# Scores of the 129-key row block in 64x128 tiles, and an earlier wait for the scores made ahead

## What is computed

```python
xn = layernorm(x, g_in)
q = (xn @ Wq).reshape(b, n, H, DH).transpose(0, 2, 1, 3) * scale
k, v = split(xn @ Wkv)
k = concatenate([nk, k]); v = concatenate([nv, v])      # 129 keys
sim = einsum('bhid,bjd->bhij', q, k) + bias             # the scores
sim = where(causal_mask, neg, sim)
attn = softmax(sim)
out = einsum('bhij,bjd->bhid', attn, v).reshape(b, n, INNER) @ Wo
return layernorm(out, g_out)
```

## Time and profile before

| | us |
|---|---|
| median of 3 runs | 2392.63 |
| lowest and highest run | 2391.18, 2395.41 |
| the profiled execution's own time | 2398.92 |
| span of its trace, first to last instruction | 2397.1 |
| PE busy | 2148.4 (90%) |
| PEld busy | 1914.7 (80%) |
| DVE busy | 1624.3 (68%) |
| ACT busy | 1557.8 (65%) |
| POOL busy | 1030.0 (43%) |
| mean granted clock of PE | 0.957 |

### The profile page before, as it was taken

One profiled execution on the slowest core, in us unless ns is written; L12 is line 12 of the kernel. 1 busy time (PEld: TensorE's weight loads), 2 busy tenths in 40 slices (PEclk: granted clock), 3 DMA queues, 4 the chain that ended last, 5 costly groups with the idle time before them and its releaser, 6 DMA issues.

```text
span 2397.1 us, 72132 instructions
## 1 busy us (share of the span) xinstructions
PE 2148.4 (90%) x26395; PEld 1914.7 (80%) x26395; DVE 1624.3 (68%) x3422; ACT 1557.8 (65%) x6241; POOL 1030.0 (43%) x1510
## 2 busy tenths in 40 slices
PE   5898988899988989888999889899899998898987
PEld 4787887788877878877888778778788887787876
DVE  5776766666766767666666666676666666676775
ACT  4676666666666766666666666666666666666765
POOL 3444444444444444444444444444444444444443
PEclk8899999999999999999999999999999999999999
DMA  7121222221222212222212211222122122211211
GB/s 244 50 58 54 63 60 59 63 60 53 58 69 58 57 52 65 57 59 63 60 53 58 69 59 53 55 58 65 59 59 65 53 58 64 59 57 53 69 49 51
DMA packets 183286, 151.60 MB, mean 63 GB/s; under 512 B 121440, under 2 KB 125616, under 8 KB 182992
## 3 DMA queue, kind: packets, MB, share of 16 engines
q1 hardware_dynamic: 181248, 145.77, 20.7%
q0 software_dynamic: 688, 1.14, 0.3%
q10 hardware_dynamic: 1056, 0.00, 0.0%
HBM read 98.56 MB, written 37.77 MB: 57 GB/s over the span
## 4 chain that ended last, share of the span: by engine, by line
PE 84%; issue 8%; DVE 2%; ACT 2%; SPq 1%; POOL 1%; DMA 1%; DVEq 0%; POOLq 0%; ACTq 0%
PE psum L708 31%; PE psum L615 17%; PE psum L581 12%; PE psum L673 9%; PE psum L691 7%; PE psum L543 3%; PE psum L632 2%; PE psum L592 2%; DVE bn_in L1072 1%; SPq L386 1%; ACT qp L870 1%; POOL probs L1474 1%; POOL masked_bias L1464 0%; ACT ln_in L839 0%; ACT probs L900 0%
## 5 line engine op out<-in xcount | busy, mean ns | idle before, releaser
L900 ACT ACTIVATE probs<-probs,neg_max 128x129 f32<-128x129 f32 (+3 forms) x2048 | 712.1, 351 | 76.3 <-DVE neg_max L1140 76.2
L1464 POOL TENSOR_TENSOR masked_bias<-bias,pad_neg 128x516 f32<-128x516 f32 (+3 forms) x512 | 404.1, 821 | 349.0 <-DVE probs L1134 345.3
L1474 POOL TENSOR_TENSOR probs<-probs,den_inv 128x512 f32<-128x512 f32 (+3 forms) x512 | 367.8, 739 | 250.3 <-DVE den_inv L1145 250.3
L1134 DVE TENSOR_TENSOR probs<-psum,masked_bias 128x648 f32<-128x648 f32 x256 | 213.0, 832 | 313.3 <-PE psum L673 312.8
L1486 POOL TENSOR_TENSOR y_out<-y_out,res 128x512 f32<-128x512 f32 x128 | 164.6, 1286 | 554.5 <-ACT y_out L864 554.5
L900 ACT ACTIVATION_READ_ACCUMULATOR probs<-probs,neg_max 128x1 f32 x2048 | 385.9, 188 | 0.0
L1150 DVE STREAM_TRANSPOSE probs_t<-probs 128x512 f32<-128x512 f32 (+3 forms) x512 | 229.9, 487 | 147.3 <-POOL probs L1474 146.3
L708 PE MATMUL psum<-wo_hi,o_hi 128*128 128x512 f32 x1024 | 307.0, 447 | 3.6 <-issue 2.1
L906 ACT ACTIVATE o_hi<-psum,null_v_col 128x512 fp32r<-128x512 f32 x256 | 161.9, 683 | 196.2 <-PE psum L691 196.2
L673 PE MATMUL psum<-keys,q_t 64*64 64x129 f32 (+3 forms) x4096 | 129.6, 265 | 156.0 <-issue 152.9
L708 PE MATMUL psum<-wo_hi,o_lo 128*128 128x512 f32 x1024 | 262.5, 398 | 0.0
(11 more groups left out here) (133 smaller groups left out, 4077.0 us busy)
## 6 DMA issues: line engine op xcount, KB each, us to landing
res<-in_x_dram SPq DMA_DIRECT2D x64, 256.0 KB, 2.8
v_rep<-v_kept SPq DMA_DIRECT2D x512, 32.0 KB, 1.8
x_of<-y_out SPq DMA_DIRECT2D x64, 256.0 KB, 2.1
res<-x_of SPq DMA_DIRECT2D x64, 256.0 KB, 2.8
out_dram<-y_out SPq DMA_DIRECT2D x64, 256.0 KB, 2.1
xa<-in_x_dram SPq DMA_DIRECT2D x63, 256.0 KB, 2.8
xa<-x_of SPq DMA_DIRECT2D x63, 256.0 KB, 2.8
q_aside<-qp SPq DMA_DIRECT2D x32, 256.0 KB, 3.0
```

Of the source, the lines that this page charges most:

```text
L900: x_ = nc.scalar.activation(s, s, ACT.Exp, bias=neg_max[:, b, n:n + 1], accum_out=den[:, b, n:n + 1])
L1134: nc.vector.tensor_tensor(pairs(probs, c), SB[c][:, :, 0:ROW], pairs(masked_bias, c), ALU.add).then_inc(biased[c], 1)
L1464: m = nc.gpsimd.tensor_tensor(block(masked_bias, b), block(bias[u.layer], b), pad_neg[u.layer][:, 0:WIDTH[b]].unsqueeze(1).to_broadcast([P ...
L1474: m = nc.gpsimd.tensor_tensor(some, some, den_inv[:, b, :].unsqueeze(2).to_broadcast([P, 4, n]), ALU.mult)
```

## The change

Block 3, of 129 keys, is made with all 128 partitions of the output at once, in two 64 x 128 tiles (one for each e) instead of four of 64 x 64; the other blocks stay. And `scores(u, 0)` of a layer-0 unit waits for `half_copied[k]` to reach `u.pfirst`, the count after the pair's first half, instead of `u.pdone * 2`, the count after both halves. `pfirst` is a new field of `Unit`, 2p + 1 for pair p. Layer-1 units and `scores(u, 1)` wait as before.

```diff
-    def __init__(self, layer, batch, done, prev, before, xdone, xprev, sdone, odd=None, pdone=None, adone=None):
-        self.before = before
+    def __init__(self, layer, batch, done, prev, before, xdone, xprev, sdone, odd=None, pdone=None, pfirst=None, adone=None):
+        self.before, self.pfirst = before, pfirst
...
-        return Unit(0, b, u + 1, u, u - 1, n + 1, n, b + 1, odd=b % 2, pdone=b // 2 + 1)
+        return Unit(0, b, u + 1, u, u - 1, n + 1, n, b + 1, odd=b % 2, pdone=b // 2 + 1, pfirst=b // 2 * 2 + 1)
...
-            return Unit(0, two[k], ..., odd=k % 2, pdone=one[k // 2 + 1])
+            return Unit(0, two[k], ..., odd=k % 2, pdone=one[k // 2 + 1], pfirst=two[k // 2 * 2 + 1])
...
                         for k in range(2):
-                            wait(pe, half_copied[k], u.pdone * 2)
+                            wait(pe, half_copied[k], u.pfirst)
                         wait(pe, k_high_loaded, u.pdone * 16)
...
                 for b in (3, 2, 1, 0):
-                    for r in range(0, P, TR):
+                    tr = P if b == BLOCKS - 1 else TR
+                    for r in range(0, P, tr):
                         for e in range(2):
                             half = slice(e * DH, (e + 1) * DH)
                             k = keys[half, 0:WIDTH[b]] if u.layer else (kv_t, k_high)[e][half, u.odd, 0:WIDTH[b]]
-                            m = nc.tensor.matmul(block(SB[c][:, e, :], b)[r:r + TR, :], queries(u, c, half, b)[:, r:r + TR], k,
+                            m = nc.tensor.matmul(block(SB[c][:, e, :], b)[r:r + tr, :], queries(u, c, half, b)[:, r:r + tr], k,
                                                  start=True, stop=True)
```

More of the change, by code:

```diff
@@ L98, in a @@
             x = 2 * k - 3 - k % 2
-            return Unit(0, two[k], four[2 * k - 1], four[2 * k - 2], four[2 * k - 3], four[x + 1], four[x], two[k + 1], odd=k % 2, pdone=one[k // 2 + 1])
+            return Unit(0, two[k], four[2 * k - 1], four[2 * k - 2], four[2 * k - 3], four[x + 1], four[x], two[k + 1], odd=k % 2, pdone=one[k // 2 + 1], pfirst=two[k // 2 * 2 + 1])
         def b(k):
```

## The result

| | before | after |
|---|---|---|
| median of the runs | 2391.94 us (4 runs, 2391.18 to 2395.41) | 2194.74 us (4 runs, 2191.74 to 2195.6) |
| after / before, 95% interval | | 0.9171 (0.9155 to 0.9187) |
| span of the trace | 2397.1 us | 2192.3 us |
| one round of the loop | 73.36 us (mean of 28) | 65.97 us |
| mean granted clock of PE | 0.957 | 0.988 |

The trace of before is of an execution of 2398.92 us, 7 us above the median, so what is summed up over its rounds comes out some us too large for the median. The chain's shares by engine, from the page of after, answer rows 1: "issue" fell from 8% to 1%.

A forecast was written before the change was run, and what follows sets the result against it. The prediction took TensorE's queue, 84% of the chain, to bound the kernel, with "issue" another 8%. Its terms summed to 2392.6 - 38 - 24 - 22 + 15 = 2324 us, range 2298 to 2374.

The forecast's parts named there:

- The weaker wait: Scores of the pair's even unit in `second`: no more waiting for q's second half, 1.30 us, 29 times: -38 us.
- Rival (3): The removed wait for q is replaced by another, the bias sum or a DMA: 2361 us, chance 0.04.
- The stall inside a call: Mid-call of scores in the loop: instruction packet ends move to slower stretches, so PE's stall goes: -24 us.
- The jump at the loop's end: Loop's end to top: the top's packet comes sooner, saving 0.8 us a round, bounds 0 and 1.3: -22 us.
- Rival (2): Packets do not move as counted, the stall is taken up elsewhere, the jump stays: 2370 us, chance 0.12.
- The clock, counted as nothing: What PE's clock does after a shorter gap at the loop's end was not counted: no term in the sum.
- The tiles: Block of 129 keys: longer 128-column first load, +0.06 us in each of 256 calls, no pause taken: +15 us.
- rival (1): Every call of scores also pays the pause between tilings: +53 us instead of +15, 2361 us, chance 0.22.

The follow-up runs named there:

- e5: The kernel before with 150 idle semaphore increments on PE ahead of all its work, nothing else changed: 2204.47 us, ratio 0.9218.
- e6: The kernel before with the weaker wait alone (all scores in 64x64 tiles) and 150 idle semaphore increments ahead on PE: 2165.33 us, ratio 0.9049.
- e2: The changed kernel with the old wait for both halves of q, so the 64x128 tiles alone: 2236.34 us, ratio 0.9347.
- e1: The changed kernel with all scores back in 64x64 tiles, so the weaker wait alone: 2364.91 us, ratio 0.9891.
- e7: The changed kernel with 170 idle semaphore increments on PE ahead of all its work: 2465.25 us, ratio 1.0312.
- e8: The changed kernel with 64x128 tiles only in the seven calls of scores ahead of the loop, 64x64 in and behind it: 2148.98 us, ratio 0.897.
- e3: The changed kernel with 88 idle semaphore increments on PE ahead of all its work: 2198.56 us, ratio 0.9189.
- e9: The changed kernel with all four row blocks, not only the widest, in 64x128 tiles: 2207.47 us, ratio 0.9217.

## Why the prediction was wrong, step by step

- **The weaker wait, -38 us: right where the loop stays with PE.** e5 and e6, which differ by it alone, differ by 39.1 us, e2 and after by 41.6, and after's list has no wait for `qp` and none in its place. Rival (3) falls. In e1, where the loop is still fetched, the median fell by 28.6 us only.
- **The stall inside a call, -24 us: near in size by luck, wrong in its reason.** Against e5 it costs 0.65 us a round, 28 x 0.65 = -18 us; the 24 came out of 28 x 4.65 us for the jumps, whose mean is 4.77. The stall is gone, but not because its packet end was moved beside slower products: no packet comes in the loop of after between 180 and 2000 us. e1, where the loop is still fetched, keeps it (1.17 us in the round shown). e7's second gap, 1.4 to 2.4 us, too lies where a packet ends by the count, 29 instructions into the round and within a call of scores.
- **The jump at the loop's end, -22 us: the step that failed.** 4.77 us became 0.10, both on the mean: 28 x 4.67 = -131 us. I assumed that the loop would be fetched each round as before and asked only where its packets would end. A sign of it was in reach: rows 7 have 278 packets, nine a round, and a round fills 6.7. That one question, why a loop is fetched at all, was not asked. The 0 to 1.3 us a round, worked out from the two packets of rows 9, bounded the wrong thing. Rival (2) had the right doubt, that the packets don't move as counted, with the wrong sign.
- **The clock, counted as nothing: -59 us.** It was set aside in one sentence. The profile of before showed it: granted clock 0.57 in the 3.2 us behind the gap, and work there that took 1.07, 1.04 and 4.56 us, against 0.82, 0.59 and 3.74 for the same pieces in e5, where the clock is 1.00 (from 921.5 to 925 us, and on the mean of 200 to 2000): 1.5 us in that round, up to 2.8 in others (1.41, 1.04 and 5.53 us). On the mean of the 28 rounds behind a jump, PE takes 6.15 us from its first product to its 49th in before and 4.05 in e5, which makes 28 x 2.10 = -59 us; from there to the end of the round only the stall differs. With the jump's 4.67 and the stall's 0.65 these 2.10 us make up the 7.43 between a round of before (73.36) and one of e5 (65.93). That all of the 2.10 us is the clock is read from the granted clock in this stretch; no run held the clock up and left the gap.
- **The tiles, +15 us: mis-sized, rival (1) was right.** A call costs 0.95 instead of 0.75 us. The parts are those of the prediction near their upper bounds: the longer first load (the second pass comes 0.21 us after the first, 0.16 in rows 11), the pause of 0.10 us and the load behind it, with 0.13 us between the passes of the 97-key block. I took no pause from rows 13, where 128 columns give way to 16 without one. That row doesn't carry over to 64x128 and 64x64, and why it shows no pause is not known; the rows that did were those of the change of rows, in rows 11, which has 0.10 us from 128x128 to 64x64 as after has from 64x128 to 64x64. e8 against after gives the price in this kernel, 46 us rather than 256 x 0.20 = 51 (1.40 us a round rather than 1.60): where the calls are short, PE waits for ACT's `o_hi` (7.5 us in 33 waits in e8, 0.9 us in after, 0.2 us a round), which after's longer calls cover.

With the measured terms the sum is -38 - 18 - 131 - 59 + 46 = -200 us; -197 was measured. Without the tiles it is -246, and e8 gained 248 on the before of its own run.

So the change pays for a reason that is not in what it is said to do. Its wide tiles lose 46 us as products. Eight instructions fewer in each call, seven calls of them ahead of the loop, move the loop to where it stays with PE (25 packets for 278), which is worth about 208 us; the weaker wait gives the other 38. e8 shows that the earlier start of the loop is enough by itself. Its shorter round would be too, an estimate from the table (113 + 1641 = 1754, and e8 and e3, which end at 1762 and 1786, stay); it was not run.

## What to carry to other kernels

Look at the count of instruction packets before anything else when a loop shows "issue" at its end. Here 278 packets, nine a round, went with a gap of 4.77 us at the mean jump (before), and 25 with one of 0.10 (after); 56 instructions fewer ahead of the loop (e8), or 150 idle ones more (e5), made the difference. Before crediting an edit with its gain, shift the loop by idle instructions alone: here 82 of them more (e7 against e3) cost 12%, with nothing changed in the loop. Price a gap with the slow work that follows it: here each 4.77 us had 2.10 us more behind it, with the granted clock at 0.50.

## What was not expected of the hardware

- A round of 1705 or 1641 instructions costs PE 0.10 us at its jump on the mean when it stays (after, e3, e8), and 3.7 to 5.1 us when it is fetched anew (before, e1, e7), with a second gap at a packet's end inside a dense stretch, of 0.3 to 1.1 us in before and 1.4 to 2.4 in e7.
- The same loop at two places: 2198.56 us (e3) and 2465.25 us (e7), 12% apart.
- With an idle stretch of 4.5 to 5.0 us at each jump, PE's granted clock in before fell from 1.00 to 0.50 at all 28, inside the gap or just behind it, so that it is the work behind the gap that runs slowly; with 0.10 us between rounds, in after, it is 1.00 from 200 to 2000 us.
- In e9 loads of 64x128 tiles follow each other by 0.11 us and set the pace of the products of 33 to 97 columns; in after, the first load of 64x64 tiles starts 0.10 us after the last product of 64x128 has streamed.
- 150 to 170 increments at PE's start delay the first transposes to 24 to 27 us, some 0.16 us each, and the loop by 12.5 to 18.5 us.
